# Spreading the reciprocals of the softmax denominators: VectorE's copy or GpSimd's

## The chip, the cores and the metric

The kernel runs on one core of one Trainium2 chip. The metric is the device time of one launch in microseconds (us). Before the change it is 1750.57 us, the median of three runs (1750.45 to 1750.68).

## The reference

The input `x` is 8 images of 56 x 56 tokens with 256 channels. It is normalized in groups of 8 channels per image, goes through a bi-level routing attention, and is added back. Cut to what matters:

```python
qkv = jnp.einsum('nchw,oc->nohw', xc, qkv_w) + qkv_b[None, :, None, None]
q, k, v = jnp.split(qkv, 3, axis=1)
# 7 x 7 regions of 8 x 8 tokens; each region takes the 4 regions whose mean key fits its mean query
a_r = q_r @ k_r
_, idx_r = jax.lax.top_k(a_r, TOPK)
key_g = jnp.take_along_axis(ks_[:, :, None], idx, axis=3)
val_g = jnp.take_along_axis(vs[:, :, None], idx, axis=3)
attn = jnp.einsum('bhnqd,bhnkd->bhnqk', qs * SCALE, key_g)     # 64 queries, 256 keys, 8 heads of 32
attn = jax.nn.softmax(attn, axis=-1)
out = jnp.einsum('bhnqk,bhnkd->bhnqd', attn, val_g)
lepe = jax.lax.conv_general_dilated(v, lepe_w, ..., feature_group_count=DIM)   # 3 x 3, depthwise
out = jnp.einsum('nchw,oc->nohw', out + lepe + lepe_b, out_w) + out_b
```

## The kernel before

**Tiling.** The 8 images have 56 rows of regions and 392 regions. The main loop goes over steps `s` (0 to 56, one for each row of regions) and in a step over seven places `rc`; the region is `r = 7 s + rc`. While region `r` is in its softmax, the same stretch of time also projects q, k and v of later rows, convolves the row `s + 1` (16 outer taps per row on VectorE, the middle tap on GpSimd), and projects the output of row `s - 1`. Steps are of five kinds: in each image one "first" (7 in all) and one "last" (7), the others "full" (23) or "short" (12: half of the output projection of some rows is put off), and the "tail" (the last seven that have regions), which does the halves that were put off. In the tail GpSimd loads the rows that were put off back into SBUF (`load_late` at places 3 to 5, `load_late_x`, three of them, at place 6), for use in the step that follows.

**The order** is written out by hand on each engine, and each engine works in its order; semaphores alone tie the engines together. For region `r`:

- TensorE: transposes the first half of the probabilities of `r`, waits for all four exponentials of `r`, makes the scores of `r + 1` (`scores`, L1098), multiplies probabilities and values of `r - 1` (`attend`), transposes the second half, does projections, then `turn_recips(r)` (L1135): it transposes the tile `recips`, which holds the reciprocals of `r` spread over 32 columns for each head; then more projections.
- VectorE: `invert(r)` (reciprocals of 128 x 4 denominators, L845), `spread(r)` (the copy to 128 x 128, L851), the two maxima of `r + 1` (L840), `normalize_o(r - 1)` (L858), and then taps (L737), statistics or output halves (`out_half`, L828; `late_half`, L835, which waits for a transfer that `load_late_x` started).
- ScalarE: evacuates PSUM banks, makes four exponentials of `r + 1` (L617), copies the transposed reciprocals (L628).
- GpSimd: `gather_keys(r + 2)` (four copies of 128 x 128, L382; there are two slots, so it waits until the scores of `r` are made, and the scores of `r + 2` wait for it), `take_region(r - 2)` (L393, adds the attention output to the convolution), then one of: a middle tap (L404), halo copies (L416, L420), `normalize` (L442), and DMA issues. Before the first region of each row it loads 28 region numbers into registers (`TENSOR_LOAD`, L285, inside `gather_keys`); as it looks two regions ahead, this falls at place 5 of the step before.

Of the kernel before, what the change touches and what calls it, by code (L numbers as in the profile page):

```python
# [11 lines left out]
P = 128  # L12
NB, H, W, C = 8, 56, 56, 256
HEADS, HD = 8, 32
# [7 lines left out]
HG = P // HD  # L22
# [42 lines left out]
def is_row(n):  # L65
    return 0 <= n < ROWS


def is_region(r):
    return 0 <= r < ALL  # L70
# [12 lines left out]
def late_rows(s):  # L83
    return [g for i in LATE_AT.get(s, ()) for g in LATE_GROUPS[i]]
# [51 lines left out]
def attention_kernel(nc, x, w_qkv, w_out, b_qkv, b_out, w_tap, b_tap, ident_d, group_d, v_dram, spill, out):  # L136
    place, early_chunks = chunk_places()

    with ExitStack() as ctx:
        def sb(name, shape, dt=F32):  # L140
            return ctx.enter_context(nc.sbuf_tensor(name, shape, dt))

        def sem(name):
# [25 lines left out]
        recips = sb("recips", [P, HG, HD])  # L169
# [3 lines left out]
        rdenom = sb("rdenom", [P, 2, HG])  # L173
# [50 lines left out]
        scores_done, max_done, exp_done, inv_done, o_normed = map(  # L224
            sem, ("scores_done", "max_done", "exp_done", "inv_done", "o_normed"))
        recips_done, recips_turned, recips_evac = map(sem, ("recips_done", "recips_turned", "recips_evac"))
# [140 lines left out]
        def _(pool):  # L367
            key_regions = {}

            def gather_keys(r):  # L370
                b = r // NREG
                if r % NREG == 0:
                    pool.wait_ge(idx_in, 16 * (b + 1))
                    wait_taken(pool, "k", b * NWIN + LAST, 0)
                    wait_taken(pool, "k", b * NWIN + LAST, 1)
                if r % NWIN in GROUPS:
                    key_regions.update(chosen(mybir.EngineType.Pool, r, GROUPS[r % NWIN]))
                reg = key_regions.pop(r)
                if r >= K_SLOTS:
                    pool.wait_ge(scores_done, r - K_SLOTS + 1)  # L380
                for j in range(TOPK):
                    last = pool.tensor_copy(k_sel[:, r % K_SLOTS, :, RT * j:RT * (j + 1)],  # L382
                                            k_all[:, b % 2, :, bass.ds(reg[j] * RT, RT)])
                last.then_inc(k_sel_done, 1)

            def take_region(r):
                g, rc = divmod(r, NWIN)
                pool.wait_ge(o_normed, r + 1)
                if rc == 0:
                    pool.wait_ge(lepe_rows, g + 1)  # L390
                cols = slice(RS * rc, RS * (rc + 1))
                cells = lepe[:, :, g % LEPE_RING, :].rearrange("p k (r c) -> p k r c", c=W)[:, :, :, cols]
                pool.tensor_tensor(cells, o_norm[:, r % 2, :].rearrange("p (k r c) -> p k r c", k=KC, r=RS), cells,  # L393
                                   ALU.add).then_inc(o_row_done, 1)
# [32 lines left out]
            def load_x(n):  # L427
                if n >= X_RING:
                    for kind in ("k", "q"):
                        for k in range(KC):  # L430
                            wait_full(pool, kind, n - X_RING, k)
                pool.dma_start(xn[:, :, n % X_RING, :], x[n]).then_inc(x_loaded[n % X_RING], 16)
# [28 lines left out]
            def spill_row(g):  # L461
                pool.wait_ge(o_row_done, NWIN * (g + 1))
                pool.dma_start(spill[LATE.index(g)], lepe[:, :, g % LEPE_RING, :]).then_inc(spilled, 16)
# [44 lines left out]
            for s in range(STEPS):  # L508
                rr, kv, xr = s % NWIN, s + KV_LEAD, s + STAT_LEAD
                for rc in range(NWIN):  # L510
                    r = s * NWIN + rc
                    if is_region(r + 2):
                        gather_keys(r + 2)
                    if is_region(r - 2):
                        take_region(r - 2)

                    if rc == 0 and is_row(s + LOAD_LEAD):
                        load_x(s + LOAD_LEAD)
                    elif rc == 1 and is_row(s + MID_LEAD):
                        mid_tap(s + MID_LEAD, 0)  # L520
                    elif rc == 2:
                        if is_row(s + MID_LEAD):
                            mid_tap(s + MID_LEAD, 1)
                        if s - 1 in LATE:
                            spill_row(s - 1)
                    elif rc == 3:
                        if rr == LAST and is_row(xr):
                            image_rstd(xr // NWIN)
                        if rr and is_row(kv):
                            halo(kv)  # L530
                    elif rc == 4 and is_row(s + NORM_LEAD):
                        normalize(s + NORM_LEAD, 1)
                    elif rc == 5:
                        if is_row(s + NORM_LEAD):
                            normalize(s + NORM_LEAD, 0)
                        if is_row(s):
                            load_resid(s)
                    elif rc == 6:
                        if is_row(s - 1):
                            store_row(s - 1)  # L540
                        if rr == 0 and is_row(kv):
                            halo(kv)

                    if rc == 1:
                        for i in LATE_AT.get(s - 1, ())[1:]:
                            store_late(i)
                    elif rc == 3:
                        for i in LATE_AT.get(s, ())[:1]:
                            store_late(i)

                    if rc >= 3 and late_rows(s + 1)[rc - 3:rc - 2] and rc < 6:
                        load_late(late_rows(s + 1)[rc - 3])
                    elif rc == 6:
                        for g in late_rows(s + 1)[:3]:
                            load_late_x(g)
                    elif rc < 2 and late_rows(s)[rc + 3:rc + 4]:
                        load_late(late_rows(s)[rc + 3])
                        load_late_x(late_rows(s)[rc + 3])
# [153 lines left out]
        def _(dve):  # L712
# [129 lines left out]

            def invert(r):
                dve.wait_ge(exp_done, HG * (r + 1))
                dve.reciprocal(rdenom[:, r % 2, :], denom[:, r % 2, :]).then_inc(inv_done, 1)  # L845

            def spread(r):
                dve.wait_ge(inv_done, r + 1)
                if r:
                    dve.wait_ge(recips_turned, r)  # L850
                dve.tensor_copy(recips[:], rdenom[:, r % 2, :].unsqueeze(2).to_broadcast([P, HG, HD])  # L851
                                ).then_inc(recips_done, 1)

            def normalize_o(r):
                if r >= 2:
# [40 lines left out]
            for s in range(STEPS):  # L896
# [3 lines left out]
                for rc in range(NWIN):  # L900
                    r = s * NWIN + rc
                    if is_region(r):
                        invert(r)
                        spread(r)
                    if is_region(r + 1):
                        maximum(r + 1, 0)

# [435 lines left out]
```

## Time and profile before

| | |
|---|---|
| median of three runs | 1750.57 us |
| the profiled execution: time of its own | 1755.16 us |
| its span, from first to last instruction | 1753.4 us |
| granted TensorE clock, mean | 0.996 |
| busy: TensorE matmuls / weight loads | 1692.8 us (97%) / 1368.0 us (78%) |
| busy: VectorE | 1524.4 us (87%) |
| busy: ScalarE | 1460.4 us (83%) |
| busy: GpSimd | 1155.3 us (66%) |
| a full step (30.2 to 30.4 us) or a short one (28.3 us) has seven regions | 4.0 to 4.4 us a region |

Busy shares alone do not tell what a microsecond on one engine is worth: the four engines hand each region around in a ring, and which of them is last differs from place to place in a step. The chain of the page (the work that ended last, followed back) and the idle time before an instruction tell that.

### The profile page before, as it was taken

What the parts mean: (1) busy time and instruction counts of PE and PEld (TensorE: products, weight loads), DVE (VectorE), ACT (ScalarE), POOL (GpSimd) and SP (SyncE); (2) the same over time, 40 slices, a digit from 0 to 9 for tenths busy, and PEclk for the clock granted to TensorE, in tenths of its full rate; (3) what the DMA queues carried; (4) which work ended last, traced back from release to release, by engine and by line L of the source; (5) the groups of instructions that cost most, each with busy time, mean ns of one, the idle gap of its engine ahead of it and who ended that gap; (6) DMA issues with size and microseconds to landing.
All of it is one profiled execution on the core that took longest, in us unless ns stands there. A gap on an engine that the chain in (4) does not pass through costs nothing.

```text
span 1753.4 us, 76313 instructions
## 1 busy us (share of the span) xinstructions
PE 1692.8 (97%) x26568; PEld 1368.0 (78%) x26568; DVE 1524.4 (87%) x3329; ACT 1460.4 (83%) x4793; POOL 1155.3 (66%) x2548
## 2 busy tenths in 40 slices
PE   4999999999999999999999999999999999999997
PEld 4878887877878778778778778787778887777775
DVE  6578989898898899988998898989988888899984
ACT  1488888888888888888888888888888888888775
POOL 3256666677666766776767676667766666577773
PEclk9999999999999999999999999999999999999999
DMA  5323434344443444343444443434443334466574
GB/s 187 90 83 112 146 109 142 113 137 125 124 131 118 133 130 132 120 136 116 136 122 132 126 135 115 140 105 147 124 124 104 112 107 124 132 196 209 179 238 162
DMA packets 164649, 234.61 MB, mean 134 GB/s; under 512 B 19232, under 2 KB 146912, under 8 KB 164272
## 3 DMA queue, kind: packets, MB, share of 16 engines
q1 hardware_dynamic: 141408, 129.71, 25.4%
q0 software_dynamic: 22864, 100.02, 17.2%
q8 instruction: 219, 3.59, 0.9%
q14 instruction: 158, 1.29, 0.2%
HBM read 166.80 MB, written 62.85 MB: 131 GB/s over the span
## 4 chain that ended last, share of the span: by engine, by line
PE 64%; ACT 18%; DVE 12%; issue 4%; DMA 1%; SPq 0%; POOL 0%; POOLq 0%; ACTq 0%; DVEq 0%
PE chunk_bank L1011 17%; ACT probs L617 14%; PE pt_bank L1111 13%; PE s_bank L1098 13%; PE o_bank L1125 8%; DVE neg_max L840 6%; PE chunk_bank L1025 6%; DVE lepe L737 4%; PE chunk_bank L1053 2%; ACT probs_t L624 2%; PE o_bank L1135 1%; PE s_bank L1011 1%; ACT v_stage L589 1%; PE chunk_bank L1073 1%; ACT q_all L598 1%
## 5 line engine op out<-in xcount | busy, mean ns | idle before, releaser
L617 ACT ACTIVATE probs<-s_bank,neg_max 128x256 f32<-128x256 f32 x1568 | 738.1, 483 | 158.0 <-DVE neg_max L840 157.7
L840 DVE TENSOR_REDUCE neg_max<-s_bank 128x2 f32<-128x512 f32 x784 | 505.9, 685 | 135.7 <-PE s_bank L1098 134.0
L737 DVE SCALAR_TENSOR_TENSOR lepe<-v_band,taps,lepe 128x448 f32<-128x448 f32 x896 | 610.4, 726 | 0.0
L382 POOL COPY k_sel<-k_all 128x128 f32 x1568 | 409.9, 304 | 283.6 <-PE s_bank L1098 268.6
L1011 PE MATMUL chunk_bank<-xn,wqkv 128*128 128x224 f32 x2544 | 570.3, 356 | 2.5 <-DVE xn L773 2.5
L624 ACT COPY probs_t<-pt_bank 128x512 f32<-128x512 f32 x784 | 466.2, 595 | 62.9 <-PE pt_bank L1111 62.8
L1111 PE MATMUL pt_bank<-ident,probs 128*128 128x128 f32 x3136 | 493.1, 280 | 0.1
L1011 PEld LDWEIGHTS chunk_bank<-xn,wqkv 128*128 128x128 f32 x2544 | 442.1, 192 | 9.1 <-DVE xn L773 2.6
L1111 PEld LDWEIGHTS pt_bank<-ident,probs 128*128 128x128 f32 x3136 | 359.0, 141 | 52.9 <-ACT probs_t L624 0.8
L393 POOL TENSOR_TENSOR lepe<-o_norm,lepe 128x128 f32<-128x128 f32 x392 | 248.2, 633 | 158.4 <-DVE o_norm L858 157.0
L617 ACT ACTIVATION_READ_ACCUMULATOR probs<-s_bank,neg_max 128x1 f32 x1568 | 332.2, 212 | 0.0
L1125 PEld LDWEIGHTS o_bank<-probs_t,v_sel 128*32 128x32 f32 x12544 | 193.4, 110 | 153.0 <-issue 149.6
L1098 PE MATMUL s_bank<-k_sel,q_all 32*64 32x256 f32 x6272 | 270.6, 400 | 18.3 <-ACT probs L617 4.5
L1125 PE MATMUL o_bank<-probs_t,v_sel 128*32 128x64 f32 x12544 | 256.8, 222 | 2.4 <-DMA v_sel<-v_dram 2.0
L1098 PEld LDWEIGHTS s_bank<-k_sel,q_all 32*64 32x64 f32 x6272 | 92.0, 130 | 93.1 <-ACT probs L617 57.1
L404 POOL TENSOR_SCALAR lepe<-v_band,taps,btap 128x448 f32<-128x448 f32 x112 | 160.4, 1432 | 0.0
L1025 PE MATMUL chunk_bank<-lepe,wout 128*128 128x224 f32 x696 | 150.9, 353 | 1.0 <-POOL lepe L393 1.0
L442 POOL TENSOR_SCALAR xn<-xn,rstd,shift 128x448 f32<-128x448 f32 x96 | 122.1, 1272 | 12.3 <-DVE shift_sum L801 12.3
L1025 PEld LDWEIGHTS chunk_bank<-lepe,wout 128*128 128x128 f32 x696 | 123.5, 190 | 2.3 <-POOL lepe L393 1.2
L851 DVE COPY recips<-rdenom 128x128 f32<-128x128 f32 x392 | 106.3, 271 | 13.4
L628 ACT COPY recips_t<-o_bank 128x128 f32<-128x128 f32 x392 | 113.4, 289 | 0.4 <-PE o_bank L1135 0.3
L1135 PE MATMUL o_bank<-ident,recips 128*128 128x128 f32 x392 | 108.2, 276 | 4.6 <-DVE o_norm L858 3.6
(77 smaller groups left out, 1304.3 us busy)
## 6 DMA issues: line engine op xcount, KB each, us to landing
v_sel<-v_dram SPq DMA_DIRECT2D x1568, 64.0 KB
xn<-x_dram POOLq DMA_DIRECT2D x56, 448.0 KB, 4.8
v_dram<-v_stage SPq DMA_DIRECT2D x112, 224.0 KB
resid<-x_dram POOLq DMA_DIRECT2D x31, 448.0 KB, 4.2
out_dram<-resid POOLq DMA_DIRECT2D x31, 448.0 KB
spill<-lepe POOLq DMA_DIRECT2D x25, 448.0 KB, 3.6
xn<-spill POOLq DMA_DIRECT2D x25, 448.0 KB, 6.5
resid<-x_dram POOLq DMA_DIRECT2D x25, 224.0 KB, 3.3
```

The costliest lines, as they stand in the source:

```text
L382: last = pool.tensor_copy(k_sel[:, r % K_SLOTS, :, RT * j:RT * (j + 1)], k_all[:, b % 2, :, bass.ds(reg[j] * RT, RT)])
L393: pool.tensor_tensor(cells, o_norm[:, r % 2, :].rearrange("p (k r c) -> p k r c", k=KC, r=RS), cells, ALU.add).then_inc(o_row_done, 1)
L404: pool.tensor_scalar(in_image(lepe[:, k, n % LEPE_RING, :]), v_band[:, n % BANDS, k, 1:1 + RS, 1:1 + W], taps[:, k, MID_TAP:MID_TAP + 1], ...
L617: act.activation(probs[:, u, :], s_bank[:, u, 0:KEYS], ACT.Exp, bias=neg_max[:, r % 2, u:u + 1], accum_out=denom[:, r % 2, u:u + 1]).then_ ...
L624: act.copy(probs_t[:, r % 2, hf, :], pt_bank[:, :]).then_inc(probs_t_evac, 1)
L737: ins = dve.scalar_tensor_tensor(row, v_band[:, n % BANDS, k, t // 3:t // 3 + RS, t % 3:t % 3 + W], taps[:, k, t:t + 1], row, ALU.mult, AL ...
L840: dve.tensor_reduce(neg_max[:, r % 2, 2 * hf:2 * hf + 2], s_bank[:, 2 * hf:2 * hf + 2, 0:KEYS], AX.X, ALU.max, negate=True).then_inc(max_d ...
L1011: ins = pe.matmul(bank_of(kind, n, k)[:, cols], wqkv[:, part, col:col + P], xn[:, part, n % X_RING, cols], start=(part == 0), stop=(part = ...
L1025: ins = pe.matmul(bank_of("out", g, m)[:, cols], wout[:, part, P * m:P * (m + 1)], lepe[:, part, g % LEPE_RING, cols], start=(part == 0), ...
L1098: last = pe.matmul(s_bank[RT * k:RT * (k + 1), u, 0:KEYS], q_all[s, g % Q_RING, k, rc, :], k_sel[s, r % K_SLOTS, k, :], start=True, stop=True)
L1111: t = pe.transpose(pt_bank[:, at:at + P], probs[:, u, P * c:P * (c + 1)], ident[:])
L1125: last = pe.matmul(o_bank[HD * u:HD * (u + 1), RT * k:RT * (k + 1)], v_sel[:, r % V_SLOTS, c, HD * head:HD * (head + 1)], probs_t[:, r % 2 ...
```

## The change

The copy `spread(r)` leaves VectorE's order. GpSimd makes it, as the first thing in its work for region `r`, ahead of `gather_keys(r + 2)`. It waits there for `inv_done` (the reciprocals of `r`) and `recips_turned` (TensorE has read the tile's last contents). VectorE's `invert(r)` gets a wait of its own, that the copy of region `r - 2` has read its slot.

```diff
+            def spread(r):
+                pool.wait_ge(inv_done, r + 1)
+                if r:
+                    pool.wait_ge(recips_turned, r)
+                pool.tensor_copy(recips[:], rdenom[:, r % 2, :].unsqueeze(2).to_broadcast([P, HG, HD])
+                                 ).then_inc(recips_done, 1)
...
                 for rc in range(NWIN):
                     r = s * NWIN + rc
+                    if is_region(r):
+                        spread(r)
                     if is_region(r + 2):
                         gather_keys(r + 2)
...
             def invert(r):
                 dve.wait_ge(exp_done, HG * (r + 1))
+                if r >= 2:
+                    dve.wait_ge(recips_done, r - 1)
                 dve.reciprocal(rdenom[:, r % 2, :], denom[:, r % 2, :]).then_inc(inv_done, 1)
-
-            def spread(r):
-                dve.wait_ge(inv_done, r + 1)
-                if r:
-                    dve.wait_ge(recips_turned, r)
-                dve.tensor_copy(recips[:], rdenom[:, r % 2, :].unsqueeze(2).to_broadcast([P, HG, HD])
-                                ).then_inc(recips_done, 1)
...
                         invert(r)
-                        spread(r)
```

Line numbers of the changed kernel differ: the copy is L390 there, `take_region` L400, `normalize` L449, `load_resid` L458, `store_row` L466, `load_late_x` L489, the reciprocal L856, the maxima L849.

VectorE at the head of two regions of a step, before:

```order
L845 RECIPROCAL rdenom<-denom 128x4 [waits exp_done]
L851 COPY recips<-rdenom 128x128 [waits recips_turned,inv_done]
L840 TENSOR_REDUCE neg_max<-s_bank 128x2 [waits scores_done] x2
L858 TENSOR_TENSOR o_norm<-o_bank,recips_t 128x128 [waits attn_done,o_row_done]
L737 SCALAR_TENSOR_TENSOR lepe<-v_band,taps,lepe 128x448 [waits lepe_step] x2
```

The same place in the changed kernel:

```order
L856 RECIPROCAL rdenom<-denom 128x4 [waits recips_done,exp_done]
L849 TENSOR_REDUCE neg_max<-s_bank 128x2 [waits scores_done] x2
L862 TENSOR_TENSOR o_norm<-o_bank,recips_t 128x128 [waits attn_done,o_row_done]
L746 SCALAR_TENSOR_TENSOR lepe<-v_band,taps,lepe 128x448 [waits lepe_step] x2
L837 SCALAR_TENSOR_TENSOR resid<-chunk_bank,bout,resid 128x448 [waits chunk_full0]
```

The copy between the reciprocal and the maxima is gone, and nothing else on VectorE moved.

GpSimd around place 5 of a step, before (`ISA` sets an address register for the copy behind it, here with the wait for the scores):

```order
L442 TENSOR_SCALAR xn<-xn,rstd,shift 128x448 [waits x_read,scale_ready]
L285 TENSOR_LOAD idx_row
L382 ISA [waits scores_done]
L382 COPY k_sel<-k_all 128x2x64
...
L393 TENSOR_TENSOR lepe<-o_norm,lepe 128x2x8x8 [waits o_normed]
L442 TENSOR_SCALAR xn<-xn,rstd,shift 128x448 [waits x_read,scale_ready]
L451 DMA resid<-x_dram 128x896
```

And in the changed kernel:

```order
L449 TENSOR_SCALAR xn<-xn,rstd,shift 128x448 [waits x_read,scale_ready]
L390 COPY recips<-rdenom 128x128 [waits recips_turned,inv_done]
L285 TENSOR_LOAD idx_row
L382 ISA [waits scores_done]
L382 COPY k_sel<-k_all 128x2x64
...
L400 TENSOR_TENSOR lepe<-o_norm,lepe 128x2x8x8 [waits o_normed]
L449 TENSOR_SCALAR xn<-xn,rstd,shift 128x448 [waits x_read,scale_ready]
L458 DMA resid<-x_dram 128x896
L390 COPY recips<-rdenom 128x128 [waits recips_turned,inv_done]
```

The register load, and all that stands behind it, now stands behind a wait for VectorE's reciprocals of region `r`.

GpSimd at place 6 of a tail step in the changed kernel:

```order
L382 COPY k_sel<-k_all 128x2x64
L400 TENSOR_TENSOR lepe<-o_norm,lepe 128x2x8x8 [waits o_normed]
L466 DMA out_dram<-resid 128x896 [waits chunk_free0,chunk_free1]
L489 DMA k_all<-x_dram 128x448 [waits late_stored2] x3
L390 COPY recips<-rdenom 128x128 [waits recips_turned,inv_done]
```

The three transfers of `load_late_x` stand between the copies of two regions, where before no instruction in GpSimd's order waited for the reciprocals.

## Rows read from the trace of the kernel before

**Rows 1.** The page: shares of the span in the chain that ended last.

```profile
PE 64%; ACT 18%; DVE 12%; issue 4%; DMA 1%; SPq 0%; POOL 0%; POOLq 0%; ACTq 0%; DVEq 0%
```

**Rows 2.** The waits: engine, line, whom it waited for: total us, times, longest.

```profile
POOL k_sel L382 <- PE s_bank L1098: 268.6, 304, 5.4
...
DVE neg_max L840 <- PE s_bank L1098: 134.0, 299, 8.8
...
PEld o_bank L1135 <- issue: 15.7, 37, 0.9
```

**Rows 3.** The page's groups by line: the copy that moves (busy us, mean ns | idle).

```profile
L851 DVE COPY recips<-rdenom 128x128 f32<-128x128 f32 x392 | 106.3, 271 | 13.4
```

**Rows 4.** Timeline (start us, us), place 6 to place 0 of a short step.

```profile
979.19 2.66 DVE L737 SCALAR_TENSOR_TENSOR lepe<-v_band,taps,lepe 128x448 f32<-128x448 f32 x4
...
981.07 0.69 PE L1098 MATMUL s_bank<-k_sel,q_all 32*64 32x256 f32 x16 [0.15 <-ACT probs L617]
981.78 0.17 DVE L845 RECIPROCAL rdenom<-denom 128x4 f32<-128x4 f32 x1
...
982.12 0.68 DVE L840 TENSOR_REDUCE neg_max<-s_bank 128x2 f32<-128x512 f32 x1
```

**Rows 5.** GpSimd by line: gather's copies, register load, normalization (ns min/median/max).

```profile
L382 POOL COPY k_sel<-k_all x1568: 279/293/771, 86.4 to 1727.3; 128x128 f32 x196
...
L285 POOLq TENSOR_LOAD <-idx_row x56: 1777/1787/3120, 84.2 to 1698.6; - x56
...
L442 POOL TENSOR_SCALAR xn<-xn,rstd,shift x96: 708/1182/1786, 110.2 to 1501.6; 128x448 f32<-128x448 f32 x96
```

**Rows 6.** Timeline, places 5 and 6 of a full step.

```profile
972.61 0.16 DVE L845 RECIPROCAL rdenom<-denom 128x4 f32<-128x4 f32 x1
...
974.90 2.07 DVE L737 SCALAR_TENSOR_TENSOR lepe<-v_band,taps,lepe 128x448 f32<-128x448 f32 x3
...
976.99 0.69 PE L1098 MATMUL s_bank<-k_sel,q_all 32*64 32x256 f32 x16
977.09 0.23 DVE L851 COPY recips<-rdenom 128x128 f32<-128x128 f32 x1
977.79 1.29 DVE L840 TENSOR_REDUCE neg_max<-s_bank 128x2 f32<-128x512 f32 x2 [0.47 <-PE s_bank L1098]
...
979.39 0.14 PEld L1135 LDWEIGHTS o_bank<-ident,recips 128*128 128x128 f32 x1
```

**Rows 7.** Timeline of the tail: a gather that lies beside taps.

```profile
1557.94 1.77 POOL L382 COPY k_sel<-k_all 128x128 f32 x4 [0.76 <-issue]
```

**Rows 8.** Timeline of a tail step, place 5 to place 1 of the next.

```profile
1559.69 0.45 POOL L393 TENSOR_TENSOR lepe<-o_norm,lepe 128x128 f32<-128x128 f32 x1
...
1560.09 0.57 POOL L451 DMA_DIRECT2D resid<-x_dram  x1
1560.09 0.17 DVE L845 RECIPROCAL rdenom<-denom 128x4 f32<-128x4 f32 x1
...
1562.15 2.07 DVE L737 SCALAR_TENSOR_TENSOR lepe<-v_band,taps,lepe 128x448 f32<-128x448 f32 x3
1563.66 1.61 POOL L482 DMA_DIRECT2D k_all<-x_dram  x3
1563.95 0.69 PE L1098 MATMUL s_bank<-k_sel,q_all 32*64 32x256 f32 x16
...
1571.53 0.69 DVE L835 SCALAR_TENSOR_TENSOR k_all<-chunk_bank,bout,k_all 128x448 f32<-128x448 f32 x1
...
1572.72 0.69 DVE L840 TENSOR_REDUCE neg_max<-s_bank 128x2 f32<-128x512 f32 x1 [0.16 <-PE s_bank L1098]
```

**Rows 9.** The line of `load_late_x`: from issue to landing, 25 transfers.

```profile
DMA to landing us min/median/max: 4.7/6.0/6.9
```

**Rows 10.** Timeline, the tail's first boundary: issue, and the instruction that reads.

```profile
1538.04 1.61 POOL L482 DMA_DIRECT2D k_all<-x_dram  x3
...
1543.59 0.68 DVE L835 SCALAR_TENSOR_TENSOR k_all<-chunk_bank,bout,k_all 128x448 f32<-128x448 f32 x1
```

## The prediction

> **What bounds the kernel now.** I read the chain of waits on the page first, then the waits by engine, then timelines of single regions. The chain is 64% TensorE, 18% ScalarE, 12% VectorE and 0% GpSimd [rows 1]: no engine is the bound alone. In a region the four hand work around in a ring: scores on TensorE, maxima on VectorE, exponentials on ScalarE, and then the next scores. So VectorE's copy costs something only where VectorE is the last to be ready for the maxima. The waits say how seldom that is: of 392 regions, the first maximum was held up by the scores in 299 [rows 2]. There the copy lies in a gap and is free. The timeline of a full step shows such a region: the copy ends at 977.32 and the maximum starts at 977.79, 0.11 us after the scores end (976.99 + 0.69) [rows 6]. GpSimd is not in the chain because it runs ahead: it stood waiting for scores 304 times, 268.6 us in total [rows 2], before a gather that nobody needs for a region and a half. The reader should keep that gap in mind, since the change spends it.
>
> **What is removed.** 392 copies, 106.3 us busy, 271 ns each [rows 3]. At most places the cover is the wait for the scores, so the gain is nothing. Where VectorE comes late it is real: at place 0 of a short step four taps run until 981.85, the reciprocal starts at 981.78, the maximum at 982.12, though the scores ended at 981.76 [rows 4]. Without the copy the maximum could start 0.11 us after those scores, at 981.87, as it does where it is on time: 0.25 us won, and then the scores are what is late. How many such places there are is read from TensorE, which then has to wait, with the transposition of the reciprocals, for the normalization behind the late maximum: the trace puts 37 waits of this kind down to "issue" [rows 2]. Upper end: 37 x 0.25 = 9.3 us. Lower end: nothing, because GpSimd's later gather (below) holds up scores at some of the same places. I take 4 us, a little under half.
>
> **What is added.** 392 copies on GpSimd. No row shows GpSimd spreading columns; the nearest is its copy of the same 128 x 128 size, 279 ns at the least and 293 in the median [rows 5], and I take 0.3 us; the addition of the same size took 0.45 us [rows 8], the upper end. When GpSimd is free the copy ends some 0.1 us later than VectorE's did, and TensorE wants it 2.07 us after that (977.32 to 979.39) [rows 6]. So the copy itself costs nothing, and its length hardly matters. The new wait in `invert` looks two regions back and costs nothing either.
>
> **What is moved.** GpSimd's order now has, at the head of each region, a wait for that region's reciprocals. Queued behind it are the gather for `r + 2`, the addition, the taps and normalizations, all DMA issues of GpSimd, and the register load at place 5. GpSimd can no longer run ahead; everything happens about a region later. For most places that is good: the gather falls beside the maxima of `r + 1`, as the one of `r + 3` did before, where a copy takes 0.28 to 0.29 us [rows 5], 1.1 us for the four, and it is done some 2 us before the scores of `r + 2`. Two places are not good.
>
> *The register load.* It takes 1.79 us [rows 5] and was hidden while GpSimd waited for scores. Now it starts when the reciprocals of place 5 are ready: 972.77, plus 0.1 for the semaphore, plus 1.79, plus some 0.2 for the address registers, gives a gather from 974.87 on. That is the moment at which VectorE's three taps start (974.90 to 976.97) [rows 6]. Beside taps the gather is slow: 1.77 us for four copies [rows 7], up to 771 ns for one [rows 5], because a copy that comes while a tap runs waits for its end. With two copies through in time it ends beside the second tap, at 976.4; with none, 0.2 us after the third, at 977.2. The scores of the next step need it at 976.99 less 0.1 [rows 6]. The stall is thus 0 to 0.3 us a step; I take 0.15. For 35 full and short steps: 5.3 us (0 to 10.5). First steps have two taps there and escape. In seven last steps scores are made nearer to the exponentials, so the gather is later against them; the maxima were late there anyway: 0.3 us each, 2 us (0 to 4), an estimate from the same rows. The Trainium skill ("DMA: Bandwidth & Descriptors", Latency and other measured facts) gives a floor of about 600 ns for such a load. By it the gather would start 1.2 us sooner and this term would vanish; no load in this trace is under 1.78 us, and this one brings 28 registers, so the row decides.
>
> *The tail.* Here the ring paces the regions (the maximum at 1572.72 waits for the scores [rows 8]), so each stall counts in full. At place 5 the reciprocals are ready at 1560.26; the gather starts at 1562.35, just behind the start of the first of three taps (1562.15 to 1564.22), and ends near 1564.5. Before, the scores were at 1563.95 [rows 8]: 0.6 us of stall. Behind the gather come the addition (0.45), two DMA issues (0.57 each at the least) [rows 8]: 1566.1. Then the spread of place 6 (0.3), its gather with two copies held up by taps (1.8) [rows 7], the addition (0.45) and a store's issue (0.57) [rows 8]: the three transfers of `load_late_x` are issued at 1569.2, and not at 1563.66, 5.5 us later. They land 6.0 us after their issue [rows 9], at 1575.2. But VectorE read the first of them at 1571.53 [rows 8], and it does so in its order: behind the read stand the reciprocals of place 1 and the maxima of place 2. From the read to that maximum VectorE needs 0.69 + 0.17 [rows 8, 4]; it started 1.19 after the read (1572.72) [rows 8], so about 0.35 us of the delay of 3.7 us is spare. Cost: 3.3 us at each of five boundaries between tail steps, 16.5 us; the 0.6 us is contained in it. At the first boundary the transfers were issued late already, 1538.04 for a read at 1543.59 [rows 10], and by the same count move by some 3.4 us; landing in 4.7 us [rows 9] they cost about 2.2 us. The last has no taps before its read and more to spare: 2.3 us. Together 21 us. The ends: landing in 4.7 us and one copy less held up leaves 2.0 us at each of the five and 1 us at the other two, 12 us; landing in 6.9 us [rows 9] and all copies held up, 4.3 us and 3 us, 27.5 us.
>
> **The sum.** -4 + 5.3 + 2 + 21 = 24.3 us, made against the profiled execution's own 1755.16 us (span 1753.4): 1779.5 us. The median of the runs shown is 4.6 us lower, 1750.57, so the forecast in its terms is 1774.9, say 1775 us. Its own bounds: -9.3 + 0 + 0 + 12 = +3 us and 0 + 10.5 + 4 + 27.5 = +42 us, 1754 to 1793.
>
> **The rivals.**
>
> *GpSimd keeps pace* (faster). The register load is over sooner, or is taken up ahead of the wait; the gather stays beside the maxima, and the late transfers move by only 3 us (reciprocals of place 6 at 1564.3, a region of 4.0 us after the 1560.26 of place 5, then 0.1 + 0.3 + 1.1 + 0.45 + 0.57, issue at 1566.8 [rows 5, 8]). They would land at 1572.8, 1.3 us late, 0.9 of it beyond the spare: 0.9 x 5 + 0.5 = 5 us. Against that the whole 9.3 us: -4 us, 1746 us (1744 to 1752). For it: GpSimd is busy only 66% of the time. Against it: order; a load that stands behind a wait cannot start ahead of it. A load of the length that the Trainium skill gives as a floor (same page and section) would lead here. 0.15, half of it within 0.2%.
>
> *The late transfers are not late* (slightly slower). GpSimd's slips cost in the ordinary steps and in the scores of the tail (7 x 0.6 = 4), but the transfers land in time because a stretched tail gives them emptier queues: -4 + 5.3 + 2 + 4 = +7 us, 1758 us (1752 to 1764). For it: the quickest landing is 4.7 us, 1.3 under the median [rows 9]. Against it: even so they come 2.4 us after the time of the read. 0.12.
>
> *The slip does not heal* (much slower). If after place 5 GpSimd is so late that the spread of place 6 comes after 979.39 [rows 6], TensorE stands at `turn_recips` as well, in every step. I find it ready at 979.2 at the latest (gather to 977.2, addition 0.45 [rows 8], the shortest normalization 0.71 [rows 5], DMA issue 0.57 [rows 8], copy 0.3), so the margin is 0.2 us or more; a normalization of the median length would use it up. With 0.7 us more in each of 49 steps: +34 us on top, 1809 us (1793 to 1825). 0.08.
>
> **How the numbers follow.** Forecast 0.65, keeping pace 0.15, not late 0.12, not healing 0.08. A difference of 0.2% (3.5 us) is about what a measurement of this kernel can tell from none. Faster than 1747: 0.07, from the first rival. Within: 0.08 from it and 0.03 from the low ends of the forecast and of the second rival, 0.11. Slower: 0.82. The range of 8 in 10 is the forecast's own without its last microsecond or so below, 1754 to 1793; it takes in most of the second rival and leaves out the first and the third, 0.2 or a little more.
>
> **What would show it.** In the changed kernel's profile: the waits should show scores (L1098's line) held up by GpSimd's gather, tens of times, a few tenths each, at places 5 to 0; the read of the late transfers on VectorE (L844) should show an idle time of 2 to 4 us put down to a DMA, seven times; the steps before the tail should each last within 0.3 us of what they did, and the tail's six full steps 31 us and not 28. The gather's copies should have a higher median at place 5 only. VectorE's busy time should fall by some 100 us and the span should not follow. The prediction is wrong if the register load's end lies ahead of the taps, if the late transfers land before their read, or if `turn_recips` becomes what TensorE waits for.

## The result and the profile after

The changed kernel takes 1781.06 us (median of four runs, 1780.28 to 1782.48) beside 1750.51 us for the kernel before: a ratio of 1.0163, 95% interval 1.015 to 1.0176. The profiled execution has a span of 1779.7 us at a mean granted clock of 0.997; before it was 1753.4 us at 0.996. The medians differ by 30.6 us, the spans by 26.3. Of the kernels further down, one launch of the load ahead of the wait (3279.08 us) and one of the kernel before beside it (5598.32 us) lay far outside the rest; the ratios leave them out, and without them the two medians are 1739.92 and 1753.25 us in place of 1740.68 and 1753.66.

The page of the changed kernel, its chain, to be held against [rows 1]:

```profile
PE 61%; ACT 14%; DVE 9%; issue 8%; POOL 6%; DMA 1%; POOLq 1%; ACTq 0%; DVEq 0%
```

GpSimd, which had no share, now has 6%, and "issue" has gone from 4% to 8%. VectorE has less to do and gains nothing: it is busy for 1428.2 us, 96 us less. The waits of the changed kernel (engine, line, whom it waited for: total us, times, longest), beside [rows 2]:

```profile
POOL recips L390 <- DVE rdenom L856: 495.3, 323, 3.5
DVE neg_max L849 <- PE s_bank L1101: 252.3, 343, 8.8
...
POOL k_sel L382 <- issue: 100.2, 56, 8.1
...
PEld o_bank L1138 <- issue: 25.6, 34, 2.2
DVE k_all L844 <- DMA k_all<-x_dram: 19.9, 7, 3.4
...
PEld o_bank L1138 <- POOL recips L390: 5.1, 7, 0.8
```

GpSimd no longer waits for scores that come later; it waits for the reciprocals of the region at hand. The third line is the register load: 56 times GpSimd now stands idle for it, 1.65 us in the example below; one of the 56, of 8.1 us, lies in the prologue and was there before the change too. The fifth is the read of the late transfers.

Timeline of the changed kernel (start us, us; in brackets the idle time before and what ended it), places 5 and 6 of a full step and the head of the short step behind it, beside [rows 4, 6]:

```profile
980.72 0.16 DVE L856 RECIPROCAL rdenom<-denom 128x4 f32<-128x4 f32 x1
980.95 0.29 POOL L390 COPY recips<-rdenom 128x128 f32<-128x128 f32 x1 [1.21 <-DVE rdenom L856]
...
981.41 1.29 DVE L849 TENSOR_REDUCE neg_max<-s_bank 128x2 f32<-128x512 f32 x2 [0.53 <-PE s_bank L1101]
...
982.82 1.93 DVE L746 SCALAR_TENSOR_TENSOR lepe<-v_band,taps,lepe 128x448 f32<-128x448 f32 x3
982.89 2.25 POOL L382 COPY k_sel<-k_all 128x128 f32 x4 [1.65 <-issue]
...
985.24 0.69 PE L1101 MATMUL s_bank<-k_sel,q_all 32*64 32x256 f32 x16 [0.27 <-issue]
986.03 1.29 DVE L849 TENSOR_REDUCE neg_max<-s_bank 128x2 f32<-128x512 f32 x2 [1.19 <-PE s_bank L1101]
...
987.05 0.99 POOL L382 COPY k_sel<-k_all 128x128 f32 x4
987.43 3.08 DVE L746 SCALAR_TENSOR_TENSOR lepe<-v_band,taps,lepe 128x448 f32<-128x448 f32 x4
988.01 0.82 POOL L400 TENSOR_TENSOR lepe<-o_norm,lepe 128x128 f32<-128x128 f32 x1
989.23 0.69 PE L1101 MATMUL s_bank<-k_sel,q_all 32*64 32x256 f32 x16
990.43 0.17 DVE L856 RECIPROCAL rdenom<-denom 128x4 f32<-128x4 f32 x1
990.52 1.25 DVE L849 TENSOR_REDUCE neg_max<-s_bank 128x2 f32<-128x512 f32 x2
```

Read it downwards. The spread follows the reciprocal at once. Then the register load holds GpSimd until 982.89, just as VectorE starts three taps; the gather takes 2.25 us among them, ends at 985.14, and the scores follow 0.1 us later. **Here the step loses 0.3 us.** GpSimd is now late for place 6: the end of its gather and its addition (0.82 us, where the one of place 5 took 0.45) lie among the four taps, which take 3.08 us and not 2.66 [rows 4]. The first maximum of the next step starts 0.60 us after the scores end (990.52 less 989.92), where it was 0.36 before (982.12 less 981.76). **Here the short step behind it loses what the missing copy should have won.**

The tail, places 5 to 0, beside [rows 8]:

```profile
1577.52 2.21 POOL L382 COPY k_sel<-k_all 128x128 f32 x4 [1.66 <-issue]
...
1581.60 1.88 POOL L382 COPY k_sel<-k_all 128x128 f32 x4
...
1583.88 0.16 DVE L856 RECIPROCAL rdenom<-denom 128x4 f32<-128x4 f32 x1
...
1584.80 1.61 POOL L489 DMA_DIRECT2D k_all<-x_dram  x3
...
1586.89 0.33 PE L1138 MATMUL o_bank<-ident,recips 128*128 128x128 f32 x1 [0.45 <-POOL recips L390]
...
1590.27 0.68 DVE L844 SCALAR_TENSOR_TENSOR k_all<-chunk_bank,bout,k_all 128x448 f32<-128x448 f32 x1 [2.94 <-DMA k_all<-x_dram]
1590.87 0.17 DVE L856 RECIPROCAL rdenom<-denom 128x4 f32<-128x4 f32 x1
```

Three transfers are issued 0.9 us after the reciprocals of place 0 (1583.88), where before they were issued well ahead of them. VectorE stands for 2.94 us before it can read the first.

**Where the time went, by steps** (from the start of a step's first reciprocal to the next one's, the two traces): ordinary steps +12.9 us (full +7.9, short +3.2, first +1.1, last +0.7), the tail up to the last reciprocal +13.0, the prologue +0.4. The tail's figure is too small by some 2 to 4 us, and not because of the change. In the profiled execution of before one tail step took 33.3 us, since TensorE waited 2.4 us there for a transfer of values and then ran at a lower granted clock for 3.5 us (rows in the last section). The same step took 29.5 and 31.0 us in two kernels below (the transfers issued earlier, the load split off) that differ from the one before on GpSimd alone. That goes with the medians, which differ by 30.6 us: the profiled execution of before took 4.6 us longer than its median.

### The profile page after: what moved, and what is told of

Read it like the earlier page. It is cut to its first block, busy times and chain, and to the rows that moved or that the text cites. A ratio compares the mean times of both kernels' runs of the same rounds, so it can differ in the third digit from the quotient of the medians.

```text
span 1779.7 us, 76703 instructions
## 1 busy us (share of the span) xinstructions
PE 1695.5 (95%) x26568; PEld 1369.1 (77%) x26568; DVE 1428.2 (80%) x2937; ACT 1465.6 (82%) x4793; POOL 1109.6 (62%) x2940
## 4 chain that ended last, share of the span: by engine, by line
PE 61%; ACT 14%; DVE 9%; issue 8%; POOL 6%; DMA 1%; POOLq 1%; ACTq 0%; DVEq 0%
PE chunk_bank L1014 17%; PE pt_bank L1114 13%; PE s_bank L1101 11%; ACT probs L626 11%; PE o_bank L1128 7%; PE chunk_bank L1028 6%; DVE neg_max L849 5%; DVE lepe L746 3%; PE chunk_bank L1056 2%; POOL k_sel L382 2%; ACT probs_t L633 1%; PE o_bank L1138 1%; PE s_bank L1014 1%; POOL lepe L400 1%; POOL xn L481 1%
## 5 line engine op out<-in xcount | busy, mean ns | idle before, releaser
L849 DVE TENSOR_REDUCE neg_max<-s_bank 128x2 f32<-128x512 f32 x784 | 505.4, 685 | 252.4 <-PE s_bank L1101 252.3
L746 DVE SCALAR_TENSOR_TENSOR lepe<-v_band,taps,lepe 128x448 f32<-128x448 f32 x896 | 617.7, 735 | 0.0
L382 POOL COPY k_sel<-k_all 128x128 f32 x1568 | 465.1, 339 | 100.6 <-issue 100.2
L390 POOL COPY recips<-rdenom 128x128 f32<-128x128 f32 x392 | 115.2, 294 | 495.6 <-DVE rdenom L856 495.3
L626 ACT ACTIVATION_READ_ACCUMULATOR probs<-s_bank,neg_max 128x1 f32 x1568 | 328.4, 209 | 0.0
L400 POOL TENSOR_TENSOR lepe<-o_norm,lepe 128x128 f32<-128x128 f32 x392 | 198.0, 505 | 2.1 <-DVE o_norm L862 2.1
L862 DVE TENSOR_TENSOR o_norm<-o_bank,recips_t 128x128 f32<-128x128 f32 x392 | 110.1, 281 | 0.7 <-PE o_bank L1128 0.7
L1138 PEld LDWEIGHTS o_bank<-ident,recips 128*128 128x128 f32 x392 | 55.2, 141 | 50.9 <-issue 25.6
```

The costliest lines, as they stand in the source:

```text
L626: act.activation(probs[:, u, :], s_bank[:, u, 0:KEYS], ACT.Exp, bias=neg_max[:, r % 2, u:u + 1], accum_out=denom[:, r % 2, u:u + 1]).then_ ...
L746: ins = dve.scalar_tensor_tensor(row, v_band[:, n % BANDS, k, t // 3:t // 3 + RS, t % 3:t % 3 + W], taps[:, k, t:t + 1], row, ALU.mult, AL ...
L849: dve.tensor_reduce(neg_max[:, r % 2, 2 * hf:2 * hf + 2], s_bank[:, 2 * hf:2 * hf + 2, 0:KEYS], AX.X, ALU.max, negate=True).then_inc(max_d ...
L1138: pe.transpose(o_bank[:, P:2 * P], recips[:].rearrange("p u d -> p (u d)"), ident[:]).then_inc(recips_turned, 1)
```

## The experiments

The theory: the exposed register load is the root of both losses in ordinary steps, the wait alone (not the copy) moves the transfers in the tail, and the copy itself is free on GpSimd. The rivals: the 392 copies on GpSimd, or its lost lead, cost in themselves; or the tail is all.

### The register load ahead of the wait

```diff
+            load_keys(0)
             gather_keys(0)
...
                     r = s * NWIN + rc
+                    if is_region(r + 2):
+                        load_keys(r + 2)
                     if is_region(r):
                         spread(r)
```

`load_keys` is the register load, taken out of `gather_keys`.

> The changed kernel with GpSimd's register load for the gather of region r+2 (the 56 loads at L285, 1.78 us each) put ahead of the wait for the reciprocals of region r instead of behind it; the spread copy stays on GpSimd. Theory T1 (the load exposed behind the new wait is what makes GpSimd late at the end of a step: the scores stall of 0.3 us and the stretched taps at the next step's first place both follow from it): the ordinary steps lose their +12.9 us against the kernel before and show the gain of the removed copy, 0 to -9; the tail keeps part of its late transfers (one wait of VectorE of at most 3 us a step, 19.9 us in sum now). Time 1745 to 1762 us. Rival R1 (the 392 copies on GpSimd, or its wait at each of 378 regions, cost by themselves): the ordinary steps keep +8 or more; time 1768 to 1780 us. Rival R2 (only the tail's late transfers matter to the sum): ordinary steps unchanged, 1775 to 1781 us.

Measured: 1740.68 us, ratio to the kernel before 0.9926 (0.9909 to 0.9942): 40 us under the changed kernel, and under the kernel before too. That is 4 us below the range that was expected. The waits, and the same places as above:

```profile
POOL recips L393 <- DVE rdenom L862: 646.3, 389, 3.4
...
DVE k_all L850 <- DMA k_all<-x_dram: 3.6, 2, 2.7
```

```profile
964.45 1.00 POOL L385 COPY k_sel<-k_all 128x128 f32 x4
964.70 1.29 DVE L855 TENSOR_REDUCE neg_max<-s_bank 128x2 f32<-128x512 f32 x2 [0.54 <-PE s_bank L1107]
...
966.10 2.13 DVE L752 SCALAR_TENSOR_TENSOR lepe<-v_band,taps,lepe 128x448 f32<-128x448 f32 x3
...
968.19 0.69 PE L1107 MATMUL s_bank<-k_sel,q_all 32*64 32x256 f32 x16
...
970.39 2.46 DVE L752 SCALAR_TENSOR_TENSOR lepe<-v_band,taps,lepe 128x448 f32<-128x448 f32 x4
...
972.26 0.69 PE L1107 MATMUL s_bank<-k_sel,q_all 32*64 32x256 f32 x16
...
973.06 0.69 DVE L855 TENSOR_REDUCE neg_max<-s_bank 128x2 f32<-128x512 f32 x1
```

The idle time put down to the load (100.2 us) is gone from GpSimd's list. The gather takes 1.00 us beside the maxima, is over 0.65 us before the taps begin, and the scores come 2.7 us after it. The four taps take 2.46 us, and the maximum starts 0.11 us after the scores (973.06 less 972.95). VectorE's waits for the late transfers fall from 19.9 to 3.6 us, though nothing but the load was moved: their issue now starts 1.5 to 1.7 us ahead of the reciprocals of place 0 at all seven boundaries, where in the changed kernel it started 0.9 us behind them at six. The ordinary steps, +12.9 us in the changed kernel, are at -8.5 us; the prologue gives 3.1 us more, since the first load also moved ahead of a wait there. The copies and the lost lead, which are still in this kernel, thus cost nothing that shows, and the tail is not all.

### The wait without the copy

The kernel before, VectorE still copying, and on GpSimd only:

```diff
+                    if is_region(r):
+                        pool.wait_ge(inv_done, r + 1)
                     if is_region(r + 2):
                         gather_keys(r + 2)
```

> The kernel before, with VectorE's copy where it was, and only the wait for region r's reciprocal added at the head of GpSimd's work for region r. It tells the wait from the copy. T1 (the wait makes GpSimd start each region's gathers, taps and transfer issues late): as slow as the changed kernel or slower by the gain that is missing, 1778 to 1792 us. Rival R1 (the copy on GpSimd costs, by its 0.29 us in front of the gathers and by its hold on VectorE's taps): the wait alone is nearly free, 1751 to 1760 us.

Measured: 1785.25 us, ratio 1.0176 (1.0159 to 1.0194), no faster than the changed kernel (1.0163). Its timeline shows the same picture at the same place:

```profile
983.53 1.93 DVE L739 SCALAR_TENSOR_TENSOR lepe<-v_band,taps,lepe 128x448 f32<-128x448 f32 x3
983.59 2.25 POOL L382 COPY k_sel<-k_all 128x128 f32 x4 [3.75 <-issue]
...
985.95 0.69 PE L1100 MATMUL s_bank<-k_sel,q_all 32*64 32x256 f32 x16 [0.26 <-issue]
```

So the loss comes with the wait, and no copy on GpSimd is needed for it.

### No copy at all

The kernel before without `spread`; `recips` is set once, and `turn_recips` waits for `inv_done`. It leaves the division out.

> The kernel before with the copy of the reciprocals left out of every region: the tile of reciprocals is set once to a constant, so the division by the denominators is left out of what is computed; the turn of the tile on TensorE stays and waits for the reciprocal as before. This is the most that taking the copy off VectorE can give. T1: the copy is bound at place 0 of 27 steps or so by 0.27 to 0.34 us, so the time falls by 4 to 9 us, 1741 to 1747 us. Rival: the ring of work that binds at place 0 closes elsewhere (TensorE's turn, ScalarE's exponentials), and the time falls by less than 2 us, 1749 to 1751 us; then the change had nothing to win.

Measured: 1745.44 us, ratio 0.9949 (0.9935 to 0.9964), 8.2 us under the kernel before. There was something to win. At place 0 of the 12 short steps the first maximum starts 0.10 us after the scores (median), and not 0.36. From scores to scores, the traces give back 2.9 us there (0.24 a step), 1.7 us at the same place of the seven last steps and 2.0 us at the head of the first steps. Another 2.9 us come in the tail, but 2.5 of them in the one step that took 33.3 us before (30.8 here), and so are hardly the copy's.

### The tail's transfers issued earlier

In the changed kernel, the three `load_late_x` of place 6 go to places 2, 3 and 4 (at the first boundary all to place 4):

```diff
-                    elif rc == 6:
-                        for g in late_rows(s + 1)[:3]:
-                            load_late_x(g)
...
+                    if s + 1 == TAIL and rc == 4:
+                        for g in late_rows(s + 1)[:3]:
+                            load_late_x(g)
+                    elif s >= TAIL and rc in (2, 3, 4) and late_rows(s + 1)[rc - 2:rc - 1]:
+                        load_late_x(late_rows(s + 1)[rc - 2])
```

> The changed kernel with the tail's late input transfers (the issues at L482 that VectorE waits for in the last steps, 5.1 and 19.9 us of waits in all) put two to four places earlier in GpSimd's order; nothing else moves. T1: the waits of the tail vanish and the tail loses 10 to 13 us of what it gained, while the ordinary steps keep their +12.9 us: 1766 to 1771 us. Rival: the transfers are late for another reason than their issue (the queue, the slots they land in), or another wait of the tail takes their place: 1776 to 1781 us. Rival R2 (the tail is all): 1750 to 1758 us.

Measured: 1766.05 us, ratio 1.0067 (1.0053 to 1.0081). VectorE's wait of 19.9 us is no longer in the list; the ordinary steps keep +12.8 us. The transfers thus cost the changed kernel 17 us by the ratios (1.0163 less 1.0067). The two medians as they stand differ by 15 us, the two traces by 14. The same edit in the kernel before:

> The kernel before with only the tail's late input transfers issued two to four places earlier, by the same edit. T1: in the kernel before they were not late (no wait of VectorE for them over 1 us), so nothing moves: within 0.2% of the kernel before, 1750 to 1757 us. Rival (the early issue is a gain of its own, and what it gave back to the changed kernel was not what the change had cost): 1738 to 1746 us.

Measured: 1753.38 us, ratio 1.0009 (1.0 to 1.0019): nothing. And on top of the load ahead of the wait:

> The changed kernel with both edits: the register load ahead of the wait, and the tail's late input transfers issued two to four places earlier. With the load ahead alone VectorE's waits for those transfers are 3.6 us in sum (19.9 in the changed kernel). T1: at most these 3.6 us go, 1736 to 1741 us, against 1740.7 with the load alone. Rival (the two repairs are independent and add, 40 and 14 us): 1725 to 1730 us.

Measured: 1739.99 us, ratio 0.9933 (0.9919 to 0.9947), the same as with the load ahead alone. The two repairs do not add: with the load out of the way there is nothing left in the tail to mend.

### The gather, too, ahead of the wait

The changed kernel with `gather_keys(r + 2)` before `spread(r)`.

> The changed kernel with the copy and its wait put behind GpSimd's gather for region r+2 (load and gather both run ahead of the wait), the register load where it was. T1: the load is then ahead of the wait and the steps lose their +12.9 us; but a gather that waits for the scores of the region holds the copy back, up to the 0.07 us of slack that TensorE's turn showed in the tail, and so the gain is smaller or eaten: 1740 to 1762 us. Rival (the copy must come first, since the turn of the reciprocals on TensorE comes about 2 us behind the reciprocal): the turn waits at the 342 ordinary regions by 0.2 us or more, above 1790 us.

Measured: 1746.42 us, ratio 0.9961 (0.9948 to 0.9974). Better than the kernel before, but the gather's copies take 369 ns in the mean and not 291: 30% of their time lies beside VectorE's taps, against 5% in the kernel before (304 ns) and none with the load alone ahead. The load alone looks like the better thing to move: its interval ends at 0.9942, this one begins at 0.9948, and a second measurement of it below ends at 0.9957.

### Whose gain is it?

The load ahead of the wait gave 13 us (11 when measured again below), more than leaving the copy out (8.2 us). So the wait itself was put to the test with the load ahead and the copy still on VectorE:

> The kernel before (VectorE keeps the copy) with the wait for region r's reciprocal at the head of GpSimd's work and the register load for region r+2 put ahead of that wait. Beside the load put ahead in the changed kernel (1740.7 us) it tells whether that kernel's 13 us under the kernel before, more than the 8.2 us that leaving the copy out of the kernel before gave, are the copy's or the wait's. T1a (the wait, once the load stands ahead of it, keeps GpSimd out of VectorE's taps, and the rest is the removed copy): some 4 to 9 us under the kernel before, 1744 to 1750 us with the kernel before at 1753.7; 3 us of that are the prologue's, where the first load moves ahead of a wait. T1b (the load ahead alone makes the wait harmless, and the 13 us are the copy's place on GpSimd): equal to the kernel before or those 3 us under it, 1750 to 1757 us. Rival (the wait costs even with the load ahead, and the copy's move pays for it): 1760 us or more.

Measured: 1743.18 us, ratio 0.9949 (0.9933 to 0.9966), just under the range of T1a. The same without the wait:

> The kernel before, copy on VectorE and no new wait, with the register load taken out of the gather and put directly ahead of it, so that it moves ahead of the gather's own waits (at the first region of an image, and in the prologue) and nowhere else. It is the run with the wait added and the load ahead (1743.2 us) less the wait. T1a (the wait with the load ahead of it is itself a gain, of 5 to 8 us beyond the prologue's 3): 1748 to 1753 us with the kernel before at 1753. Rival (the gain of that run is the load's earlier place alone): 1741 to 1746 us.

Measured: 1750.86 us, ratio 0.999 (0.9981 to 0.9999), and its first reciprocal comes 3.3 us earlier than in the kernel before: this is the prologue's share. **The wait, which cost the changed kernel its loss, is worth 7 us once the load stands ahead of it** (by the ratios, whose intervals do not touch). The groups by line (busy us, mean ns | idle) show how. Without the wait:

```profile
L743 DVE SCALAR_TENSOR_TENSOR lepe<-v_band,taps,lepe 128x448 f32<-128x448 f32 x896 | 610.6, 728 | 0.0
...
L396 POOL TENSOR_TENSOR lepe<-o_norm,lepe 128x128 f32<-128x128 f32 x392 | 248.1, 633 | 155.9 <-DVE o_norm L864 154.4 <-PE chunk_bank L1059 0.4
L407 POOL TENSOR_SCALAR lepe<-v_band,taps,btap 128x448 f32<-128x448 f32 x112 | 163.8, 1463 | 0.0
...
L857 DVE COPY recips<-rdenom 128x128 f32<-128x128 f32 x392 | 109.3, 279 | 13.4
```

With it:

```profile
L745 DVE SCALAR_TENSOR_TENSOR lepe<-v_band,taps,lepe 128x448 f32<-128x448 f32 x896 | 585.4, 699 | 0.0
...
L396 POOL TENSOR_TENSOR lepe<-o_norm,lepe 128x128 f32<-128x128 f32 x392 | 178.3, 455 | 7.7 <-DVE rdenom L853 5.5 <-DVE o_norm L866 2.2
L859 DVE COPY recips<-rdenom 128x128 f32<-128x128 f32 x392 | 89.1, 227 | 13.5
...
L407 POOL TENSOR_SCALAR lepe<-v_band,taps,btap 128x448 f32<-128x448 f32 x112 | 80.2, 716 | 0.0
```

Every one of these got shorter, on both engines: the middle taps by half, VectorE's taps by 29 ns, its copy by 52 ns. The middle taps had 63% of their time beside VectorE's taps and now have 9%, GpSimd's additions 62% and now 2%. The wait puts GpSimd's gather and addition beside the maxima, and they are over when the taps begin, as the timeline of the first experiment showed. How much of the 7 us this makes is not shown. Between the two traces, which lie 4.3 us apart, the ordinary steps give 3.1 us; one tail step gives 2.3 us (31.0 to 28.7), and there TensorE's wait of 2.3 us for a transfer of values is gone; the prologue takes 1.0 us back.

Last, three kernels on one chip, all with that wait and the load ahead, that differ only in who copies:

> The changed kernel with the register load ahead of the wait, again, beside the next two on one chip: all three have GpSimd wait for the reciprocal with the load ahead of that wait, and differ only in who spreads the reciprocals. Here GpSimd does. If where the copy stands is worth something under that wait, this one lies 1.5 to 4 us under the second and at most 2 us above the third; if not, all three lie within 1.5 us.

> The same wait and the same load, with the copy on VectorE. Worth something: 1.5 to 4 us above the first, 1743 us. Worth nothing: within 1.5 us of it.

> The same wait and the same load, with the copy left out of every region and the reciprocals' tile set once to a constant, so that the division by the denominators is left out of what is computed. It is the floor for any place of the copy. The copy costs nothing on GpSimd: within 1 us of the first. It costs on GpSimd too (0.29 us ahead of every gather): 2 us or more under the first.

Measured: 1741.3 us with the copy on GpSimd (ratio 0.9943, 0.993 to 0.9957), 1744.36 on VectorE (0.996, 0.9946 to 0.9974), 1742.17 with none (0.994, 0.9926 to 0.9954). With the copy on GpSimd the median is 0.9 us lower than with none, so as far as these intervals tell (2.4 us either way) it is free there. On VectorE it costs some 2 to 3 us. The intervals of the first two overlap, so by these runs alone that is likely and not certain. The traces speak for it: against the kernel before, the ordinary steps are at -8.2 us with GpSimd's copy, -4.0 with VectorE's (and the same, -8.5 and -4.0, in the earlier pair), -7.0 with none.

## Why the prediction was right, and where it was not

The forecast was 1775 us, 24.3 us more in the profiled execution's terms; it came 6 us higher, inside the range and on the side forecast. That the sum is so near is in part luck: the traces have +12.9 us in the ordinary steps where the forecast had +3.3, and in the tail 13.0 (14 to 17 by issuing the transfers earlier) where it had 21, so two errors of opposite sign made up for each other. Point by point:

- **The chain and the ring** (the copy lies in a gap at most places): right. VectorE gave up 96 us of work and the span did not follow; without any copy the kernel gains only 8.2 us. The upper end of the gain, 9.3 us, is near that by luck: it counted 37 waits of TensorE, but only 19 of them lie at place 0 of short and last steps, and those 19 are gone without the copy. At 0.24 us each they are worth 4.6 us; the rest of the 8.2 us came elsewhere.
- **The gain of 4 us, in the ordinary steps: the step that failed.** From the end of one region's scores to the next's, place 0 to 1 lost 2.7 us in the 12 short, 1.5 in the seven last and 0.9 in four of the full steps, where the kernel without the copy had won; the first steps gained 2.9 at their head. That is a loss of some 2 us and outside the bounds of -9.3 to 0. The forecast let GpSimd's slip hold up scores alone. It overlooked that the same slip carries the gather and the addition of place 6 in among VectorE's four taps, and that they hold up the taps (3.08 us for 2.66 [rows 4]) just ahead of those places where the copy's 0.25 us was to be won.
- **The register load at place 5:** mechanism, place and even the moment were right (gather beside the taps, scores directly behind its end). The size was too low. The next step's first scores came later by 0.34 us in each of 23 full and 0.10 in each of 12 short steps, 9.1 us where 5.3 was taken (bounds 0 to 10.5), of which the interval behind gave back 0.09 a step, 3.3 us. In seven last steps it was 0.63 us, 4.4 where 2 was taken (bound 4). The 0.15 us of the forecast was the middle between two copies through in time and none: the four copies took 2.25 us, as with none. First steps escaped, as said. Together with the gain that failed this is the ordinary steps' +12.9 us where the forecast had +3.3. The load took 1.777 us at the least again. The floor that the Trainium skill gives ("DMA: Bandwidth & Descriptors", Latency and other measured facts) would have put the gather ahead of the taps; the row was right to decide.
- **The tail:** right in its mechanism, but the wait alone does not do it, since with the load ahead most of it is gone. Issue 5.4 us later against the reciprocals of place 0 (5.5 forecast), VectorE held up seven times, 19.9 us, at most 3.4. Price 14 to 17 us where 21 was taken; the transfers landed 5.7 us after issue in the median and not 6.0. TensorE's wait for the spread in the tail (5.1 us) was forecast by none of the terms.
- **The copy costs nothing on GpSimd** (0.3 us forecast, 294 ns mean, beside 271 [rows 3] on VectorE): right as far as the last three runs tell.
- **The rivals.** "GpSimd keeps pace" asked for the load to be taken up ahead of the wait, and put 1746 us on it (1744 to 1752). With the load there it is 1740.7: right side, too little, because the wait's own gain was not seen. "Not late": VectorE waited for the transfers at all seven boundaries. "Does not heal": the turn had 0.5 us to spare at place 6 of full steps (0.2 forecast), and TensorE stood for the spread only in the tail.
- **The signs it named.** VectorE's busy time, the seven reads and the tail's steps (30.4 to 31.5 us) came as said. Steps before the tail were to stay within 0.3 us; the full ones grew by 0.35 in the mean. Scores held up by the gather are not in the list of waits, which has one such wait of 4.2 us before and after. They show in this, that the scores start 0.10 us after the end of their gather (medians of full, short and last steps), where it was 1.9 to 6.6 us before. The load's end, which was to lie behind the start of the taps, lay 0.07 us behind it in full steps and 0.15 ahead of it in short ones.

That the load holds up the short steps' scores by 0.10 us and those of the full steps by 0.34 can be read from the traces. Place 5 of a short step in the changed kernel:

```profile
1009.84 0.16 DVE L856 RECIPROCAL rdenom<-denom 128x4 f32<-128x4 f32 x1
...
1010.76 1.29 DVE L849 TENSOR_REDUCE neg_max<-s_bank 128x2 f32<-128x512 f32 x2 [0.75 <-PE s_bank L1101]
...
1012.01 2.24 POOL L382 COPY k_sel<-k_all 128x128 f32 x4 [1.65 <-issue]
```

Here the reciprocals start 0.92 us ahead of the maxima; in the full step above 0.69 us (980.72 and 981.41), and before it was 0.89 to 0.90 in both kinds. In full steps the load and the gather thus start 0.2 us nearer to the scores that need them. What makes those reciprocals late was not tried by itself. It lies near that at place 4 of the full step VectorE's last tap takes 1.05 us (0.88 before) beside a normalization of 1.18 us on GpSimd, which in short steps takes 0.72.

What stays open is how the gain of the wait divides between taps that are let alone and the transfer that TensorE no longer waits for in the tail.

## What to carry to other kernels

When a step moves to an engine that "has time", look at what the new wait makes everything behind it wait for: here the copy was free, and a 1.8 us register load that had run under another wait cost 40 us against the same kernel with the load one line earlier (3 of them in the prologue). Put what does not need the awaited data ahead of the wait. And an engine that runs ahead is not free of cost to the others: when two engines slow each other down, a wait that sets the time of one of them can be worth something by itself: 7 us here, beside 2 to 3 us for the copy that was moved.

## What the runs showed of the hardware

- GpSimd and VectorE hold each other up, both ways. Four gather copies take 1.00 us beside the maxima and 2.25 us beside three taps; GpSimd's middle taps take 716 ns in the mean where 9% of their time lies beside VectorE's taps, 1463 ns where it is 63%; and VectorE's four taps at place 6 of a full step take 2.46 us with no instruction of GpSimd's data work beside them, 2.66 with 0.82 us of it (before), 3.08 with 1.54 us (changed).
- The load of 28 registers takes 1.78 us at the least and 1.79 in the median in all of these traces, and in the changed kernel GpSimd runs nothing between the copy and the gather around it: 56 loads, 100.2 us of idle time (8.1 of it in the prologue, as before) when no other wait covers them.
- TensorE's clock after a short gap. In the profiled execution of before, TensorE stood for values in the tail, and the windows around it (us, then busy time of PE, PEld, DVE, ACT and POOL with their instructions, the granted clock, DMA share and GB/s) read:

```profile
1684.00:1686.50 2.50, 0.55 (x16) 0.09 (x13) 1.74 (x5) 1.46 (x5) 1.29 (x5) 1.00 0.91 277
1686.50:1690.00 3.50, 3.46 (x41) 3.04 (x42) 1.68 (x3) 1.31 (x5) 0.82 (x1) 0.51 0.51 171
1690.00:1694.00 4.00, 4.00 (x68) 3.18 (x67) 2.82 (x7) 2.15 (x9) 1.25 (x5) 1.00 0.21 64
```

  After 2.5 us with 0.55 us of matmuls the granted clock was 0.51, the level of 1.2 GHz, for 3.5 us, and then 1.00 (2.4 GHz) again. TensorE had stood for 1.99 us between two matmuls, and the step took 33.3 us. In the kernels without the copy and with the load split off it stood there for 2.23 and 1.86 us, the granted clock stayed at 1.00, and the step took 30.8 and 31.0 us: where the clock fell, the step took 2.3 to 2.5 us more than with the gap alone.
